# A recurrent network's step on one core: each state product waits for one semaphore, ScalarE's output gate goes ahead of its second cell tanh, and VectorE queues both states ahead of their second parts

## What is computed

```python
def step(carry, xp):                      # 6250 times, one after the other; hidden size 256
    h, c = carry
    gates = xp + h @ W_hh.T               # W_hh is 1024 x 256
    i, f, g, o = jnp.split(gates, 4, axis=-1)
    c = jax.nn.sigmoid(f) * c + jax.nn.sigmoid(i) * jnp.tanh(g)
    h = jax.nn.sigmoid(o) * jnp.tanh(c)
    return ((h, c), h)
```

## Time and profile before

| | before |
|---|---|
| median of 3 runs | 18594.18 us (18592.13 to 18594.49) |
| profiled execution | 18633.15 us, of which the span of its instructions is 18631.2 us |
| PE busy | 12709.7 us (68%) |
| PEld busy | 11702.6 us (63%) |
| DVE busy | 11309.6 us (61%) |
| POOL busy | 7125.5 us (38%) |
| ACT busy | 6860.5 us (37%) |
| steps of the recurrence | 6250, from about 4080 us to 18440 us of the span |

### The profile page before, as it was taken

One profiled execution on the slowest core, in us unless ns is written; L12 is line 12 of the kernel. 1 busy time (PEld: TensorE's weight loads), 2 busy tenths in 40 slices (PEclk: granted clock), 3 DMA queues, 4 the chain that ended last, 5 costly groups with the idle time before them and its releaser, 6 DMA issues. The chain is left out here.

```text
span 18631.2 us, 977308 instructions
## 1 busy us (share of the span) xinstructions
PE 12709.7 (68%) x375188; PEld 11702.6 (63%) x375188; DVE 11309.6 (61%) x78004; ACT 6860.5 (37%) x38649; POOL 7125.5 (38%) x26609
## 2 busy tenths in 40 slices
PE   1333434557777777777777777777777777777776
PEld 1222333447777777777777777777777777777775
DVE  2333211166666666666666666666666666666666
ACT  0000100134444444444444444444444444444443
POOL 0888888403333333333333333333333333333331
PEclk9666666765555555555555555555555555555555
DMA  3444444310000000000000000000000000000000
GB/s 101 72 72 72 67 68 68 77 36 1 1 1 1 1 1 1 1 1 1 1 1 1 1 1 1 1 1 1 1 1 1 1 1 1 1 1 1 1 1 14
DMA packets 938625, 317.06 MB, mean 17 GB/s; under 512 B 750941, under 2 KB 908138, under 8 KB 938596
## 3 DMA queue, kind: packets, MB, share of 16 engines
q0 software_dynamic: 435200, 207.54, 7.4%
q1 hardware_dynamic: 503396, 109.17, 3.0%
HBM read 150.06 MB, written 150.93 MB: 16 GB/s over the span
## 5 line engine op out<-in xcount | busy, mean ns | idle before, releaser
L1233 PE MATMUL bank<-hrest,whh 128*128 128x3 bf16 (+1 forms) x300000 | 9112.1, 167 | 3342.1 <-DVE hrest L1382 3342.1
L1233 PEld LDWEIGHTS bank<-hrest,whh 128*128 128x128 bf16 x300000 | 8579.7, 104 | 3900.4 <-DVE hrest L1382 3899.8
L1338 POOL TENSOR_TENSOR part_uv<-uv,share 128x2 f32<-128x2 f32 x12500 | 2431.4, 195 | 9410.9 <-DVE uv L1374 9410.9
L1307 ACT ACTIVATE gates<-zi 128x3 f32<-128x3 f32 x12500 | 2298.9, 205 | 8068.0 <-DVE zi L1363 8068.0
L1363 DVE TENSOR_REDUCE zi<-bank 128x3 f32<-128x9 f32 x12500 | 2057.7, 167 | 2677.4 <-PE bank L1233 2677.4
L1315 ACT ACTIVATE tc<-uv 128x1 f32<-128x1 f32 x12500 | 3006.6, 288 | 0.0
L1382 DVE SCALAR_TENSOR_TENSOR hrest<-og,tc 128x1 f32<-128x1 f32 x12500 | 2009.7, 161 | 1290.0 <-ACT tc L1315 1172.3
L1340 POOL TENSOR_TENSOR gates<-part_uv 128x1 f32<-128x1 f32 x12500 | 2409.8, 193 | 980.2
L1233 PE MATMUL bank<-xsteps,wih 128*128 128x15 bf16 (+1 forms) x60048 | 2717.4, 174 | 0.0
L1311 ACT ACTIVATE og<-zo 128x1 f32<-128x1 f32 x12500 | 2433.0, 195 | 0.0
L1233 PEld LDWEIGHTS bank<-xsteps,wih 128*128 128x128 bf16 x60048 | 2284.9, 104 | 0.0
(11 more groups left out here) (171 smaller groups left out, 3792.0 us busy)
## 6 DMA issues: line engine op xcount, KB each, us to landing
ht<-acc_d SPq DMA_DIRECT2D x100, 250.0 KB
xsteps<-x_d SPq DMA_DIRECT2D x1252, 7.5 KB, 1.7
U<-hrest SPq DMA_DIRECT2D x1250, 5.0 KB, 1.7
acc_d<-zero SPq DMA_DIRECT2D x24, 796.9 KB
rows<-xn_d,staged_i POOLq DMA_INDIRECT x800, 4.0
acc_d<-sums,target POOLq DMA_INDIRECT x800, 6.1
x_d<-x SPq DMA_DIRECT2D x25, 375.0 KB, 2.3
xall<-in_x SPq DMA_DIRECT2D x5, 1250.0 KB
```

The lines of the kernel that those rows point to most:

```text
L1233: return nc.tensor.matmul(to, w, v, start=start, stop=True, skip_group_check=True)
L1307: nc.scalar.activation(gates[:, k, 0:3], zi[:, k, :], ACT.Tanh).then_inc(ifg_act[k], 1)
L1338: nc.gpsimd.tensor_tensor(part_uv[:, k, :], uv[:, k, :], share[:], ALU.mult).then_inc(cell_made[k], 1)
```

## The change

Three lists change. On ACT the output gate of half 1 goes ahead of the cell's tanh of half 1. On DVE the sum of the output gate of half 1 goes ahead of the cell terms of half 1, and the first part of half 1's state goes ahead of the second part of half 0's. The wait for the output gate (`o_act`) is dropped from `state1`, since ACT, whose results come in order, now makes that gate ahead of the cell's tanh in both halves. Nothing is added or left out of the arithmetic.

```diff
@@ scalar, order of a step
                     tanh_ifg(1)
                     tanh_o(0)
                     tanh_cell(0)
+                    tanh_o(1)
                     tanh_cell(1)
-                    tanh_o(1)
@@ vector
                     def state1(k):
-                        dve.wait_ge(o_act[k], t + 1)
                         dve.wait_ge(tc_ready[k], t + 1)
                         if s == 0 and due(16 * i):
                             dve.wait_ge(h_out[b], 16 * i)
@@ vector, order of a step
                     sum_ifg(1)
                     sum_o(0)
                     cell_terms(0)
+                    sum_o(1)
                     cell_terms(1)
-                    sum_o(1)
                     state1(0)
+                    state1(1)
                     state2(0)
-                    state1(1)
                     state3(0)
                     state2(1)
                     state3(1)
```

## The result

| | before | after |
|---|---|---|
| median | 18594.33 us (4 runs, 18592.13 to 18595.25) | 19242.55 us (4 runs, 19237.43 to 19244.69) |
| ratio, 95% interval | | 1.0348 (1.033 to 1.0366) |
| profiled execution, span | 18631.2 us | 19235.5 us |
| PE busy | 12709.7 us | 13542.5 us |
| ACT busy | 6860.5 us | 6860.1 us |

The forecast was 19340 us with a range of 19120 to 19650. The kernel became 648 us slower where 750 were forecast.

A forecast was written before the change was run, and what follows sets the result against it. The recurrence's step-by-step chain was taken as the bound. 0.11 us from B0 behind A1 plus 0.015 for PE's halt, taken as 0.12 over 6250 steps, gave 750 us: 18594 to 19340 us, 4.0% slower, range 19120 to 19650.

The forecast's parts named there:

- What bounds the kernel: Recurrence: no engine full, a chain of short work sets the time, 2.297 us a step; PE's eighth product needs B0.
- The single wait: DVE, half 0's first state part: starts 0.035 behind tc, 0.07 earlier, giving PE only its first seven products earlier.
- B0 behind A1: DVE, half 0's second state part behind half 1's first: tc to eighth product 0.64 us against 0.53, 0.11 longer.
- The halt: PE ahead of its eighth product: halts 0.17 to 0.18 us; the next product follows at 0.048, 0.015 more.
- The steps with a store's wait: DVE, 2 steps of 10: loss 0.03 to 0.07 in one, up to 0.18 in the other, mean near 0.12.
- in two pieces, 7 and 41: PE profile sign: the 48 products split so, with a new PE wait for L1386.
- split over both halves: DVE profile sign: its wait for tc would be divided between half 0 and half 1.
- the register operation isn't free: DVE, between A1 and B0: costs 0.03; the rival had it free, 0.09 a step, 19160 us, chance 0.17.
- og and tc overlap as taken: ACT: og costs 0.093; the rival kept today's 0.15 spacing, 0.175 a step, 19690 us, chance 0.12.
- no change: Rival on ACT and DVE: og and the register operation are free, 18594 to 18610 us; chance 0.03.
- faster: Rival at PE: eighth product isn't held, only the single wait counts, -437 us, 18157; chance 0.03 for over 0.2% faster.

The follow-up runs named there:

- third experiment: Kernel before with the output gate's wait dropped for half 0 alone, all orders as before: 18331.99 us, ratio 0.986.
- fifth: Changed kernel with DVE's state order of before, and GpSimd starting cell work only when both halves' cell terms are there: 18174.64 us, ratio 0.9774.
- sixth experiment: Changed kernel with GpSimd starting a step's cell work only when both halves' cell terms are there: 19245.07 us against 19242.55.
- seventh experiment: Kernel before with half 1's output gate and its sum moved ahead, both waits and DVE's state order kept: 18593.57 us, ratio 1.0.
- fourth experiment: Changed kernel with the register operation moved ahead of half 0's first state part, by a tanh count higher by one: 19069.46 us, 173 us less.
- eighth experiment: Changed kernel with DVE's state order undone, GpSimd late, and the store's wait put ahead of the step's first sum: 18164.21 us, ratio 0.9768.

## Why the prediction was right, and where its sum was off

**What bounds the kernel** held. The step's chain, the eighth product's need of B0 and PE's own pace behind it explain which way every run went: each edit that reached B0 or A0 on that path moved the time, and the two that didn't (ACT's order alone; GpSimd's delay on the changed kernel) moved it by under 3 us.

**The single wait**: 0.035 behind tc, as forecast. By itself it brings 261 us (third experiment), and together with GpSimd's delay 420 (fifth, 18594.76 - 18174.64); what the delay alone would bring, with both waits kept, no run shows. In the change it brings nothing, as the prediction said, for B0 is what PE needs.

**B0 behind A1**: og's cost on ACT was forecast at 0.093 and is 0.09 (second tc at 0.29 instead of 0.20). A1 at 0.035 behind tc: so measured. A1 to B0 was forecast at 0.108 and is 0.10: the register operation costs 0.02 and not 0.03. Over 6250 steps that term is about 60 us too high. The other terms (og, the wait, B0 to the product) were each 0.002 to 0.003 too high as well, but that is about what the sum had left out when it took 0.12 where its own terms give 0.125: there it was right by luck.

**The halt**: the eighth product starts at 10008.78 + 0.53 - 0.188 = 10009.12, which is 0.63 behind the first tc's end, where 0.64 was forecast and 0.53 stood before. The ninth is then 0.048 behind it, as forecast. In an ordinary step the loss is 0.11: A0 to A0 is 2.39 us now and was 2.28.

**A0's length** was missing in the prediction, which left it at 0.16. It became 0.19, because the early A0 starts beside a GpSimd operation (sixth experiment). So PE's first seven products came only some 0.035 earlier and not 0.07, and PE halted for 0.13 and not for 0.17 to 0.18. In the changed kernel this costs nothing; where the state order is undone it takes almost half of what the single wait is worth.

**The steps with a store's wait** are the term that was mis-sized. The prediction put "their mean near the 0.12 of the rest". The first state products of three such steps after, around one at the loop's start:

```profile
10010.92 0.44 DVE L1381 SCALAR_TENSOR_TENSOR hrest<-og,tc 128x1 f32<-128x1 f32 x2 [0.20 <-ACT tc L1315]
10013.41 0.34 DVE L1381 SCALAR_TENSOR_TENSOR hrest<-og,tc 128x1 f32<-128x1 f32 x2 [0.30 <-ACT tc L1315]
10015.72 0.43 DVE L1381 SCALAR_TENSOR_TENSOR hrest<-og,tc 128x1 f32<-128x1 f32 x2 [0.21 <-ACT tc L1315]
```

The two steps are 2.49 and 2.31 us long, 4.80 together, and two ordinary ones 4.79: a late A0 costs the kernel after nothing, for the time between A0 and A1 takes it in. The kernel before had to pay for it:

```profile
10022.44 0.16 DVE L1382 SCALAR_TENSOR_TENSOR hrest<-og,tc 128x1 f32<-128x1 f32 x1 [0.19 <-ACT tc L1315]
10024.84 0.18 DVE L1382 SCALAR_TENSOR_TENSOR hrest<-og,tc 128x1 f32<-128x1 f32 x1 [0.29 <-ACT tc L1315]
10027.14 0.16 DVE L1382 SCALAR_TENSOR_TENSOR hrest<-og,tc 128x1 f32<-128x1 f32 x1 [0.20 <-ACT tc L1315]
```

2.40 + 2.30 = 4.70, against 4.56 for two ordinary ones. So every ten steps the change gives back 0.13 us, 625 times: 81 us. With the 60 from the register operation's term the forecast of 750 becomes 609, and the spans differ by 604. The prediction had given the step with the late A0 a loss of 0.03 to 0.07 and had let the other block's make up for it with up to 0.18; measured, the first lost next to nothing, and the other no more than an ordinary step.

The medians differ by 648 and not by 604, for the profiled execution of before was 39 us slower than its median. In it PE takes longer for the 48 products in two steps of ten than in the others:

```profile
10022.66 1.49 PE L1233 MATMUL bank<-hrest,whh 128*128 128x1 bf16 x48 [0.48 <-DVE hrest L1382]
```

The seventh experiment's kernel has the same median as before and a profiled execution near it (18591.72). There the products take 1.45 us in such a step too, and a step is 2.290 us (9998.1 / 4366) instead of 2.297, which makes 42 us:

```profile
L1386 DVEq ALU_OP  x4367: 40/40/45, 5001.4 to 14999.5; - x199
```

By that kernel (A0 at 10007.28, 10009.65 and 10011.95) the steps with the store's wait give back 0.10 to 0.11 us, some 66 us, so that 750 - 60 - 66 = 624 stands against the 648 of the medians. The last 24 us are open.

**What the profile was to show**: the 48 products did not come "in two pieces, 7 and 41", and there was no PE wait for the second part. The halt of 0.13 us is covered by the seventh product's own record of 0.165, and the busy time of PE grew instead (13542.5 us against 12709.7). The sign was wrong though the halt was there; only the record's length in narrow windows showed it (0.35 to 0.53 at the eighth). DVE's wait for tc was to be "split over both halves". The list of waits has it for A0 alone (4178 times), but the idle time ahead of the state products has both:

```profile
L1381 DVE SCALAR_TENSOR_TENSOR hrest<-og,tc 128x1 f32<-128x1 f32 x8356 | 1457.0, 174 | 1212.9 <-ACT tc L1315 886.9
```

The 326 us that it puts down to nothing are A1's, 0.08 a step. The step is 2.39 us long, where 2.42 was forecast.

**Rivals**: the register operation isn't free (fourth experiment), og and tc overlap as taken, and neither *no change* nor *faster* came near. What makes a faster kernel is leaving the state order out of the change.

## What to carry to other kernels

Before queueing an instruction that waits ahead of one that is ready, ask who needs the second and when: on an engine that works in order, the ready one inherits the wait, and here its taker had only 0.01 us to spare. Drop the waits that an order already implies, above all where the semaphore that comes last would sit on an instruction of its own, but judge such a gain by the next thing that the consumer needs. And test a change of several edits one by one: here a gain of 1.4% lay under a loss of 3.5%, and another 0.9% lay in an engine that was never on the chain.

## What the hardware showed beyond that

- **Which semaphore comes last matters, not only how many there are.** With two waits A0 started 0.10 behind tc, with one 0.035. In the kernel before, the separate instruction was tc's (line 1379), the one that comes last. This wait instruction takes 0.021 us and what follows it needs some 0.045 more; if it is the late one, that is paid on the path. The eighth experiment met the same 0.07 in the sum of the gates, where the wait for PE had gone to the separate instruction, although the store's semaphore had been given long since. The Trainium skill, Perfetto Trace Analysis, section Identifying Dependency Chains, says that instructions which wait on multiple engines may have such wait instructions put ahead of them; the traces agree, and add the price.
- **GpSimd lengthens a VectorE operation that starts beside one of its own.** A0 took 0.19 to 0.20 us instead of 0.16 when a GpSimd operation had started 0.01 us before (third experiment), but 0.16 with none beginning just ahead of it (fifth and sixth experiments). In the kernel before, A0 (10011.02, 0.16 long) started 0.08 behind this one of POOL and ran beside it unharmed:

```profile
10010.94 0.19 POOL L1340 TENSOR_TENSOR gates<-part_uv 128x1 f32<-128x1 f32 x1
```

  The Trainium skill, SBUF — State Buffer, section SBUF: two separate sides, says that a VectorE operation with two SBUF inputs and a GpSimd operation that reads SBUF share a port pair, which the one that starts first holds for its whole length. The contention is here, but not its length: only some 0.03 us were lost beside an operation of 0.19 to 0.20. That it is this port is the page's word; the runs show only that GpSimd's start does it, and so that the engines of this kernel don't meet at semaphores alone.
- **A wait holds back what stands behind it even on the sequencer.** In the changed kernel A1 starts 0.28 us behind A0. All that time the register operation behind it doesn't start; none stands in the trace from 10008.40 to 10008.81, and this one starts in the window 10008.81 to 10008.83, 0.01 to 0.02 behind A1:

```profile
L1385 DVEq ALU_OP  x1: 40/40/40, 10008.8 to 10008.8; - x1
```

  Moved ahead of A0, it brought 173 us, together with the shorter B0 (fourth experiment). The Trainium skill, Perfetto Trace Analysis, section DVE / Act Engine Instruction, has the sequencer free as soon as an instruction is in the wait queue; by that the edit would have brought nothing.
